# Channel sums of an attention kernel taken by transposing sums on VectorE, with root tiles of 32 partitions, in place of matrix products with a tile of ones

## The reference

```
x = x + L0(gn(x))                    # log-sum-exp product per position, weights acc
x = x + L1(gn(x))

def L1(t):                           # t: 32 images, 1024 tokens, 128 channels
    nf = t / max(sqrt(sum(t*t, channels)), 1e-12)
    A  = softmax(5 * (nf @ adj_w @ nf.T))
    h  = A @ (t @ affine_w.T + affine_b)
    h  = (h - mean(h, channels)) / sqrt(var(h, channels) + 1e-5) * ln_g + ln_b
    return where(h >= 0, h, 0.01 * h)
```

## Time and profile before

| | |
|---|---|
| three runs | 1118.21, 1119.42, 1122.18 us; median 1119.42 |
| the profiled execution | span 1118.2 us, as the lowest of the three runs; nothing lies around the span |
| TensorE | 1034.9 us busy, 93% of the span |
| ScalarE | 911.4 us, 82% |
| VectorE | 804.3 us, 72% |
| GpSimd | 536.2 us, 48% |
| chain that ended last | PE 84%, DMA 7%, DVE 4% |

### The profile page before, as it was taken

One profiled execution on the slowest core, in us unless ns is written; L12 is line 12 of the kernel. 1 busy time (PEld: TensorE's weight loads), 2 busy tenths in 40 slices (PEclk: granted clock), 3 DMA queues, 4 the chain that ended last, 5 costly groups with the idle time before them and its releaser, 6 DMA issues.

```text
span 1118.2 us, 19802 instructions
## 1 busy us (share of the span) xinstructions
PE 1034.9 (93%) x7144; PEld 784.9 (70%) x7144; DVE 804.3 (72%) x1385; ACT 911.4 (82%) x1703; POOL 536.2 (48%) x267
## 2 busy tenths in 40 slices
PE   1199999968999999999999999999999999999994
PEld 0055555546887877777777777777777788777772
DVE  7723555578777777777777777777777777777776
ACT  1699999538888888888888888888888888888784
POOL 0044455503355555555555555555555555555543
PEclk9999999969999999999999999999999999999998
DMA  8989999730122222222322222223222222222213
GB/s 358 397 330 403 411 404 406 312 151 19 57 77 77 77 76 77 76 76 76 105 104 96 101 107 96 95 80 100 86 77 77 76 76 76 77 77 77 76 57 115
DMA packets 33421, 159.13 MB, mean 142 GB/s; under 512 B 4268, under 2 KB 4904, under 8 KB 23080
## 3 DMA queue, kind: packets, MB, share of 16 engines
q1 hardware_dynamic: 33320, 157.82, 37.1%
HBM read 136.97 MB, written 20.83 MB: 141 GB/s over the span
## 4 chain that ended last, share of the span: by engine, by line
PE 84%; DMA 7%; DVE 4%; ACT 1%; issue 1%; POOL 1%; SPq 1%; POOLq 0%; ACTq 0%; DVEq 0%
PE PS L1207 22%; PE PS L1208 21%; PE PS L1209 21%; PE PS L1225 5%; DMA Wt<-acc 4%; PE PS L1184 4%; PE PS L1174 4%; PE PS L1219 2%; PE PS L1195 2%; DMA X<-x 2%; DVE st L751 2%; PE PS L1213 2%; DMA NU<-factor_rows 0%; SPq L294 0%; PE PS L1240 0%
## 5 line engine op out<-in xcount | busy, mean ns | idle before, releaser
L928 DVE TENSOR_TENSOR Pl<-PS,Ph 128x512 fp32r<-128x512 f32 x512 | 348.1, 690 | 183.6 <-ACT PS L603 178.7
L602 ACT ACTIVATE Ph<-PS 128x512 fp32r<-128x512 f32 x384 | 235.0, 612 | 94.8 <-PE PS L1209 92.1
L603 ACT ACTIVATE PS<-PS 128x512 f32<-128x512 f32 x512 | 305.7, 611 | 7.9 <-PE PS L1209 7.9
L1207 PE MATMUL PS<-Ph,hh 128*128 128x512 f32 x512 | 206.4, 403 | 0.3 <-DVE Pl L928 0.3
L1208 PE MATMUL PS<-Pl,hh 128*128 128x512 f32 x512 | 200.0, 391 | 0.0
L1207 PE MATMUL PS<-uTh,nTh 128*128 128x512 f32 x512 | 199.9, 390 | 0.0
L1209 PE MATMUL PS<-uTh,nTl 128*128 128x512 f32 x512 | 199.6, 390 | 0.0
L1208 PE MATMUL PS<-uTl,nTh 128*128 128x512 f32 x512 | 199.6, 390 | 0.0
L1209 PE MATMUL PS<-Ph,hl 128*128 128x512 f32 x512 | 199.5, 390 | 0.0
L425 POOL TENSOR_TENSOR hl<-X,hh 128x1024 fp32r<-128x1024 f32 (+1 forms) x33 | 77.2, 2339 | 195.4 <-ACT hh L587 169.1
L408 POOL TENSOR_TENSOR LL<-LL 128x512 f32<-128x512 f32 x64 | 82.6, 1290 | 137.5 <-ACT LL L500 137.5
(11 more groups left out here) (136 smaller groups left out, 1595.5 us busy)
## 6 DMA issues: line engine op xcount, KB each, us to landing
Wt<-acc SPq DMA_DIRECT2D x64, 1024.0 KB, 7.5
out<-X SPq DMA_DIRECT2D x38, 512.0 KB, 2.6
X<-x SPq DMA_DIRECT2D x16, 1024.0 KB, 19.7
SQ<-norm_rows SPq DMA_DIRECT2D x31, 512.0 KB, 3.7
X<-factor_rows SPq DMA_DIRECT2D x31, 512.0 KB, 4.1
NU<-factor_rows SPq DMA_DIRECT2D x31, 512.0 KB, 5.0
X<-out SPq DMA_DIRECT2D x7, 512.0 KB, 5.8
out<-X SPq DMA_DIRECT2D x2, 256.0 KB, 2.4
```

The costliest lines, as they stand in the source:

```text
L602: act.activation(Ph[:, g % RING, :], sl, ACT.Exp, scale=SHARP)
L603: act.activation(sl, sl, ACT.Exp, scale=SHARP).then_inc(weights_ready, 1)
L928: dve.tensor_tensor(Pl[:, r, :], SL[r], Ph[:, r, :].bitcast(F32), ALU.subtract)\
L1207: pe.matmul(out_, lh, rh, start=start, stop=False)
```

## The change

The two sums leave TensorE. `norms` stays for images 0 and 1 and `moments` for the first half of the last image; all others go to VectorE. A `tensor_reduce` with `apply_transpose=True` turns each block of 32 partitions by 32 positions and sums over its 32 channels, so that 128 x 1024 elements give 128 x 32 sums: position i of each group of 32 on a partition, once for each of the four quarters of the channels. Three copies bring the quarters to partitions 0 to 31, a small `tensor_reduce` adds them, and all root work runs on tiles of 32 x 32 (32 x 64 for the outputs) in SBUF. A transpose on VectorE turns the result for the DMA to DRAM, which now reads 32 partitions with runs of 32 values (before: 4 partitions with runs of 256).

Slots move as well: `CAST` from (3, 7, 11, 14) to (0, 3, 11, 14); `leaky` from k 6 to k 8; `norm_roots` to k 4; the new steps at k 1 and 2 (`norm_sums`, `norm_total`), 5 (`norm_rows_out`), 6 and 15 (`output_sums`), 7 (`output_total`). `inverse_deviations` stays at k 10. In the last image the roots of image 30 move from k 6 and 7 to k 8 and 9. TensorE's waits that guarded the PSUM tiles of the sums fall away. The orders of POOL and SP do not change.

```diff
-CAST = (3, 7, 11, 14)
+CAST = (0, 3, 11, 14)
...
+            def quadrants(sums, folds, count):
+                dve.wait_ge(folds, count)
+                for g in (1, 2, 3):
+                    dve.tensor_copy(sums[0:32, g], sums[32 * g:32 * g + 32, 0]).then_inc(folds, 1)
+                dve.wait_ge(folds, count + 3)
+            def norm_sums(b):
+                dve.wait_ge(sq_ready, b + 1)
...
+                dve.tensor_reduce(n_sums[:, 0, :], ZT[b % 2].rearrange("p (k i) -> p k i", i=32), AX.X, ALU.add,
+                                  apply_transpose=True).then_inc(n2_folds, 1)
+            def norm_total(b):
+                quadrants(n_sums, n2_folds, at + 1)
+                dve.tensor_reduce(n_half, n_sums[0:32].rearrange("p g k -> p k g"), AX.X, ALU.add).then_inc(n2_folds, 1)
+                dve.wait_ge(n2_folds, at + 5)
+                dve.tensor_scalar(n_sum, n_half, NORM_MIN**2, None, ALU.max).then_inc(n2_clamped, 1)
+            def output_sums(b, e):
+                dve.wait_ge(output_taken, 4 * b + 2 * e + 2)
+                dve.tensor_reduce(q_sums[:, 0, :, e * KH:(e + 1) * KH],
+                                  pairs[b % 2][:, :, half(e)].rearrange("p t (k i) -> p t k i", i=32), AX.X, ALU.add,
+                                  apply_transpose=True).then_inc(q_folds, 1)
...
             def inverse_deviations(b):
-                y, v = rows_of(b)[:, 1, :], m[:, w:2 * w]
+                y, v, m = q_rows[:, 1, :], q_sum[:, 1, :], q_sum[:, 0, :]
...
+                dve.transpose(q_out, q_rows).then_inc(q_steps, 1)
...
-                        if k == 6 and b >= 2:
+                        if k == (1 if b else 6) and b + 2 < B:
+                            norm_sums(b + 2)
+                        if k == (2 if b else 7) and b + 2 < B:
+                            norm_total(b + 2)
+                        if k == 6 and b:
+                            output_sums(b - 1, 1)
+                        if k == 7 and b:
+                            output_total(b - 1)
+                        if k == 8 and b >= 2:
                             leaky(b - 2)
+                        if k == 15 and b < B - 1:
+                            output_sums(b, 0)
...
-                        if k == 8 and b + 2 < B:
-                            inverse_norms(b + 2)
+                        if k == (5 if b else 9) and b + 2 < B:
+                            norm_rows_out(b + 2)
...
-                        if k == 7 and b + 2 < B:
-                            norms(b + 2)
-                        if k == (7 if b < B - 1 else 5) and b:
-                            moments(b - 1)
```

More of the change, by code:

```diff
@@ L55 @@
 BACK = 10
-CAST = (3, 7, 11, 14)
+CAST = (0, 3, 11, 14)
 QR = NPOS // Q
 QH = HW // Q
+KB = NPOS // 32
+KH = HW // 32
+SUMMED = 2
 def casts_before(g):
@@ L687, in attention @@
                             values_upper(b + 1)
[L688 removed]
+                        if k == (4 if b else 8) and b + 2 < B:
                             norm_roots(b + 2)
[L690 removed]
+                        if k == 8 and b:
                             deviation_roots(b - 1)
@@ new lines, in norm_total, with norm_rows_out @@
+            def norm_total(b):
+                at = 5 * (b - SUMMED)
+                quadrants(n_sums, n2_folds, at + 1)
+                dve.tensor_reduce(n_half, n_sums[0:32].rearrange("p g k -> p k g"), AX.X, ALU.add).then_inc(n2_folds, 1)
+                dve.wait_ge(n2_folds, at + 5)
+                dve.tensor_scalar(n_sum, n_half, NORM_MIN**2, None, ALU.max).then_inc(n2_clamped, 1)
+            def norm_rows_out(b):
+                at = n2_before(b)
+                dve.wait_ge(n2_roots, 2 * b + 2)
+                dve.scalar_tensor_tensor(out=n_half, in0=n_sum, scalar=-0.5, in1=n_root, op0=ALU.mult,
+                                         op1=ALU.mult).then_inc(n2_steps, 1)
+                dve.wait_ge(n2_steps, at + 1)
+                dve.tensor_tensor(n_half, n_half, n_root, ALU.mult).then_inc(n2_steps, 1)
+                dve.wait_ge(n2_steps, at + 2)
+                dve.scalar_tensor_tensor(out=n_root, in0=n_half, scalar=1.5, in1=n_root, op0=ALU.add,
+                                         op1=ALU.mult).then_inc(n2_steps, 1)
+                dve.wait_ge(n2_steps, at + 3)
+                if b > SUMMED:
+                    dve.wait_ge(n2_kept, 16 * (b - 1))
+                dve.transpose(n_row, n_root).then_inc(n2_steps, 1)
@@ new lines, in output_sums, with output_total @@
+            def output_sums(b, e):
[3 more added lines that the diff above has]
+                                  apply_transpose=True).then_inc(q_folds, 1)
+            def output_total(b):
+                at = 6 * b
+                quadrants(q_sums, q_folds, at + 2)
+                dve.tensor_reduce(q_sum, q_sums[0:32].rearrange("p g t k -> p t k g"), AX.X, ALU.add).then_inc(q_folds, 1)
@@ L1050, in attention @@
                         if k == 14 and b == B - 1:
-                            inverse_deviations(b)
+                            last_inverse_deviations()
                 closing()
@@ L1303, in attend, with last_moments @@
                       start=m == 0, stop=m == TT - 1).then_inc(attended, 1)
[L1305 to L1315, removed]
+            def last_moments():
+                b = B - 1
+                pe.wait_ge(output_taken, 4 * b + 2)
+                pe.wait_ge(uTl_ready, 2 * B)
+                moments_into(W0, pairs[b % 2], QH).then_inc(q_made, 1)
             def opening():
@@ L1365, in attention @@
                         if k == 14 and b == B - 1:
-                            moments(b)
+                            last_moments()
                 closing()
```

123 lines of the change are left out of this document (76 added, 47 removed).

## The result

The changed kernel takes 1265.32 us (median of four runs, 1265.15 to 1269.15) where the kernel before, on the same chip, takes 1118.82: a ratio of 1.130, 95% interval 1.127 to 1.132 (the two medians alone give 1.131). The forecast was 1248 us, range 1100 to 1285. The span of the profiled execution is 1263.6 us, 145.4 more than before.

A forecast was written before the change was run, and what follows sets the result against it. VectorE was taken to become the bound: 24.5 + 2.9 + 3.6 = 31.0 us an image, +4.33 for 29 images (+126), +3 at the edges, on 1118.2: about 1247 us span, 1248 median, range 1100 to 1285.

The forecast's parts named there:

- TensorE's floor: Time an image of TensorE's remaining products, 26.67 less 1.63: 25.04 us, if VectorE keeps up.
- block at slot 10: `inverse_deviations`, operands now all in SBUF, waits for POOL's L425 or also L450: 2.4 to 3.05 us, taken as 2.9.
- block at slot 2: `norm_total`'s copies and clamp wait for POOL's L444 and L421: nothing to 4.0 us, taken as 3.6.
- VectorE without blocks: VectorE's own work an image: 20.65 less 3.55 removed, plus 3.4 for sums and 4.0 for small instructions, 24.5 us.
- edges, once: Last image: roots of image 30 come two slots later and may wait behind L450, +3 us.
- The open question of the prediction: Whether SBUF-to-SBUF copies with one input wait for POOL at slot 2; placed with the waiting ones, from per-column prices.
- The two-pass sum: Alternative of 2.26 us for each transposing sum instead of one pass, adding 3.4 us; 0.08 of the forecast's share.
- SP's queue: `put_rn` and `put_rq` stand behind the store; DMAs given their old times, with up to 0.5 us more in the range.
- rival 3: No block, but the chain through DRAM closes: 26.1 us an image, about 1105 us; chance 0.12.
- Rival 1: Only two-input operations wait for POOL, the copies pass: 27.4 us an image, about 1143 us; chance 0.17.
- Rival 2: Copies catch one POOL instruction, or slot 10 slips past L425: 28 to 29.5 us, 1160 to 1205; chance 0.14.
- Rival 4: Nothing holds VectorE, so TensorE's floor sets the time: about 1074 us; chance 0.12.

The follow-up runs named there:

- the two edits that free them: Two separate edits of the changed kernel: output moments `q_sum` put in PSUM, 1219.97 us; `norm_total` moved from slot 2 to slot 6, 1210.66 us.
- kernel at 1084.56: Changed kernel with `q_sum` in PSUM, `norm_total` at slot 6, SP's store behind the puts and loads, and `affine` moved from slot 4 to 6: 1084.56 us.
- the kernel with both edits: Changed kernel with `q_sum` in PSUM and `norm_total` moved from slot 2 to slot 6, together: 1206.44 us, ratio 1.077.
- the kernel at 1090 above: Changed kernel with `q_sum` in PSUM, copies on ScalarE, no clamp, slots kept, SP's store behind puts and loads, `affine` at slot 6: 1090.42 us.

## Why the prediction was right

The direction, the mechanism and the two places were those predicted, and the time lies 17 us above the forecast, inside its range. The range is wide, and the times of rivals 1 to 3 lie in it too, so the time alone decides little; the ends of the blocked instructions and the two edits that free them decide. By its steps:

| term, us an image | forecast | measured | where |
|---|---|---|---|
| TensorE's floor | 25.04 | 25.2 | kernel at 1084.56: 25.40 x 297.92 / 300 |
| a transposing sum, pitch | 1.13 | 1.16 | 720.45 to 721.61 |
| block at slot 10 | 2.9 | 2.5 | group means, below |
| block at slot 2 | 3.6 | 4.2 | group means, below |
| VectorE without blocks | 24.5 | 25.0 | 31.70 less 6.7 |
| an image | 31.0 | 31.70 | L470 |
| edges, once | +3 | +0.4 | 145.4 less 29 x 5.00 |

*The blocks.* At slot 10 the four operations take 0.65 + 1.98 + 0.25 + 0.38 = 3.26 us on average and 0.72 with their operand in PSUM: 2.5 us. At slot 2 three copies take 1.105 us each instead of 0.171, the clamp 1.53 instead of 0.17: 2.8 + 1.4 = 4.2. That is 0.2 above the upper bound of 4.0, which stopped at the end of L421; VectorE comes to the copies 10.55 us after the end of `inverse_deviations` (711.74 to 722.29; forecast 10.6), but POOL's L462 starts at +8.93 and not at +7.35, since the rows come back later. So the copies meet the first of the three instructions, and the clamp stays to the end of the last. Together 6.7 us where 6.5 were forecast: what one has too much the other nearly has too little, so that their sum came out this near is luck.

*The copies.* The open question of the prediction, whether a copy with one SBUF input waits for POOL, is answered: it does (1.105 us at slot 2, 0.171 at slot 6 in the same kernel but for the place). The guess from the per-column price was right in its result; that this price is the reason was not tested. The clamp, a scalar operation with one input, does the same. The sums do not: L922 takes 0.40 us beside L441, 0.37 on average, and the transposing sum 1.23 beside L462 as elsewhere. The Trainium skill, SBUF — State Buffer, section "Who interferes with whom", says that copies and scalar operations on SBUF tensors may exclude GpSimd and be excluded for a whole instruction, and that a `tensor_reduce` never contends on trn2; this trace agrees with both, with these numbers.

*VectorE's own work.* It came out 0.5 us too cheap. The two-pass sum is excluded (1.23 us). The 18 small instructions were right: where nothing blocks them, their places take 1.18 us (slot 7), 0.76 (slot 5), 1.10 (`norm_total` at slot 6 in the kernel with both edits) and 1.03 (slot 10 there) from their first start to the next instruction, 4.07 for the 4.0 forecast. Of the half microsecond the sums have 0.1 and waits for ScalarE 0.15 (4.2 us over 28 images); the rest is not resolved.

*What will show it.* TensorE was to be idle for 5 or 6 us an image; it waits 4.1 (113.5 over 28). The missing part is in TensorE's own products: after a wait of 3.03 us, for one, they start 0.43 us apart and not 0.23, and TensorE is busy for 27.5 us an image (260.53 of 300 us, times 31.70) and not 25.2, so part of VectorE's delay is covered by slower products (last section).

*SP's queue* is the step that was mis-sized. The DMAs were given their old times, with 0.5 us in reserve; the two puts take 0.8 and 1.55 us more. In the result that costs little, as forecast, since the block holds `inverse_deviations` for longer: moving the store brings 15 us while the blocks are in. But the step was wrong where it priced **rival 3**. It gave 26.1 us an image and 1105 us without blocks. With both blocks taken away and the slots kept, the chain closes at 29.3 us and the kernel takes 1196: `put_rq` leaves 2.8 us after the inverse deviations, not 1.8 (`put_rn` takes longer, and the 0.4 us for issuing `load_rn` were left out), and takes 3.45 to land, not 1.77, and slots 5 to 10 take 10.55 us with their waits, not 9.4. So the block and the chain are two bounds of nearly one height, 31.7 and 29.3 us; the blocks explain the time of the changed kernel, but by that kernel only 2.4 us an image, 70 of the 147 us lost, lie above what the chain would have cost without them.

*The other rivals.* Rival 1 fell: the copies do not pass, and its 1143 us would not have been reached either, since the kernel in which only slot 10 blocks takes 1211. Rival 2 describes single images (L1017 has a mean of 0.38 us, so the wait now and then falls on a later step), not the mean. Rival 4's floor of 1074 is nearly reached, but that needs more than was thought: no block at either place, the puts ahead of the store and `affine` two slots later give 1084.56, 25.40 us an image.

## What to carry to other kernels

Work that is moved from TensorE to VectorE in many small steps has to be placed by POOL's timeline, not only by VectorE's free time: a 0.2 us step between two SBUF tensors costs what POOL has left of its instruction, while a sum, or an operand in PSUM, costs its own length. A row that goes to DRAM and back in a closed chain should be issued ahead of large transfers on its queue, not behind them. When a kernel has several bounds of nearly one height, taking one away shows the next, so an experiment on one of them alone measures their difference and not the cost of the one.

## What the runs showed of the hardware

How long a small put holds the load that waits for it hangs on what was issued ahead of it on SP's queue. For the puts of 32 partitions in short runs, from 300 to 1000 us: 1.36 and 1.39 us in the rows of the kernel at 1090 above, where nothing had been issued for 4 us or more (single ones up to 2.6 there); 2.4 us at the least and 2.6 on average 0.4 us behind a store of 512 KB; 3.1 at the least and 3.3 to 3.4 on average 0.4 us behind a load of 512 KB. The short runs alone are not what makes it slow: with the load 1.2 to 2.8 us ahead, in the kernel at 1084.56, the put takes 1.86 us on average, and the old rows, 2.0 to 2.7 us behind theirs, took 1.81. Why a large transfer just ahead costs this much is not shown.

TensorE's products can slow down after a wait. The timeline (start, length) of the changed kernel:

```profile
729.28 0.80 PE L1307 MATMUL PS<-Ph,hh 128*128 128x512 f32 x1 [3.03 <-DVE Pl L1002]
729.87 0.63 PE L1308 MATMUL PS<-Pl,hh 128*128 128x512 f32 x1
730.30 0.63 PE L1309 MATMUL PS<-Ph,hl 128*128 128x512 f32 x1
```

In windows of 2 us the granted clock is 0.83 from 728, 0.50 from 730 (the lower of its two levels, 1.2 GHz), 0.82 from 732 and 1.00 from 734. After the wait of 1.06 us at slot 12 of the same image the products start 0.23 us apart again from the second on. It is not the rule after every long wait: at 665.89, after one of 3.29 us, they start 0.23 us apart from the second on. Of the 55 waits for VectorE's subtraction from 320 to 1200 us, 27 are followed by products 0.43 us apart, none of them among the 20 shortest (up to 1.4 us). Here the slow products cost nearly nothing of their own, because TensorE would have waited: VectorE stands only 0.15 us an image for the exponentials made from them. In the kernel at 1084.56 the clock of the steady part is 1.00.
